# A fourth block of 250 nodes through the first dense layer inside the edge loop of a GNN and expert kernel

## The chip, the core and the metric

One core of one Trainium2 chip runs the whole program. The time is the device time of one launch in microseconds (us). Three runs of the kernel before gave 595.5, 597.15 and 599.0 us, median 597.15.

## The reference

1250 nodes with 512 numbers each, 21250 edges sorted by destination (20000 drawn, and one loop per node: 17 edges a node), 64 numbers per edge. What the change concerns is the graph layer:

```python
msg = relu(x[src] + edge_attr @ W_e + b_e)          # x is layer-normalised
aggr = segment_sum(msg, dst)
h = (1.0 + eps) * x + aggr
h = silu(batchnorm(h @ W1 + b1))                    # 512 -> 1024, statistics over all nodes
h = h @ W2 + b2                                     # 1024 -> 512
h = silu(batchnorm(h))
```

The result is added to x. Then a layer norm, a softmax gate over 16 experts, for each expert its best 156 tokens, two dense layers of 512 by 512 with a gelu between them, and a weighted scatter-add follow.

## The kernel before, in words

**Ahead of the loop** the nodes are normalised, written to a table in memory (`node_rows`) and turned into columns: `aggT` holds 4 x 128 features by 1250 nodes and starts as (1 + eps) x.

**The edge loop** takes 167 tiles of 128 edges in 56 steps (0 to 55) of three tiles (`step` on each engine, `SB` = 56). For every tile POOL issues one gather of 128 source rows (line 487) into a ring of 26 rows. PE multiplies the edge attributes in float16 halves (line 1348), two tiles at a time and two pairs ahead. DVE adds the gathered row (line 982). ACT takes the Relu into `msg` (line 615). PE folds the messages into a window of 32 nodes with a one-hot matrix (line 1327, eight instructions a tile). After a step ACT copies the sum (line 593), PE turns it (line 1336) and DVE adds it into `aggT` at the window's place (line 933, "the accumulate"; that of step i is made in step i + 1). Every 3.3 steps edge attributes are rounded to their high half on ACT (line 587) and to their low half on DVE (line 955), which lets SP load the next ones.

**Blocks of the first dense layer.** Since edges are sorted by destination, the first nodes are finished early. Three blocks of 250 nodes are multiplied by W1 inside the loop. `ZSTART` names the step in which a block's columns of `aggT` are split into float16 halves: high on ACT (`part_high`, line 600), low on DVE (`part_low`, line 965), each an instruction of 1000 columns, behind the step's other work. From the next step on, in the steps of `part_at`, PE makes one product each (`part_product`, 12 matmuls of 250 columns, line 1357; one of 8 groups of 128 output features), behind the fold of the step's second tile. One step later (`ZLAG`) ACT copies it out of PSUM with the bias (line 605) and DVE takes the statistics (line 971). `ZOFF` spreads the eight products over ten steps. W1's own halves are made in the four steps from `W1_FIRST` = `ZSTART[0] - 6`.

**Whether the nodes are finished** is guarded by `SLOPE` and `OFFSET`. An assert demands ZSTART x SLOPE - OFFSET to cover the block. In the kernel, DVE compares every step's smallest destination with step x SLOPE - OFFSET (lines 859 and 868). If one is below, the loop runs 41 times instead of once.

**After the loop** the last chunk of nodes, `CH[2]`, passes the first layer: ACT rounds it (line 664), PE runs 32 high matmuls over 8 banks (line 1401) and then 64 others, feature group by feature group (line 1407). ACT copies each group out (`add_bias_1`, line 641), DVE takes statistics and combines them (`z1_statistics`, lines 1014 and 1015). In between, the halves of W2 are made (ACT line 645, DVE line 1007); SP issues W2's load when the last gathered row has been used (line 418). After five of the eight groups ACT takes a square root (line 651), DVE computes the coefficients, and the silus begin (`silu_1`, line 658). They go by chunks: eight feature groups of `CH[0]`, of `CH[1]`, of `CH[2]`. DVE splits each (`split_h1`, lines 1033 and 1035).

**The second dense layer** goes chunk by chunk, 96 matmuls each (also line 1357, in the helper `product`; operands `big` and `pair` instead of `rows_z`), 3 x 32 x (sum of columns) in all. Chunk 0 takes feature groups as they come; the other two go output by output. DVE adds the bias and takes statistics (`bias_2`, lines 1042 and 1045). The rest (second silu, gate, choice of tokens, 16 experts) begins behind the last of them.

The orders on all queues are written out by hand.

Of the kernel before, what the change touches and what calls it, by code (L numbers as in the profile page):

```python
# [22 lines left out]
def gnn_ffn_kernel(nc, E, x, src, dst, dst_rows, edge_attr, W_e, b_e, W1, b1, g1, beta1, W2, b2, g2, beta2, eps,  # L23
# [6 lines left out]
    HK = H // 128  # L30
    T = -(-E // Q)
    NP = -(-T // 2)
    SB = -(-T // J)
# [8 lines left out]
    F1 = H2 // 128  # L42
# [2 lines left out]
    KH = K // 2  # L45
    LN_EPS = BN_EPS = 1e-5
    W_SCALE = 64.0
    CH = [(0, 375), (375, 375), (750, 500)]
    ZC = 250
    ZPARTS = 3  # L50
    SLOPE, OFFSET = 21.5, 14.0
    ZSTART = (13, 24, 36)
    ZOFF = (0, 1, 2, 4, 5, 6, 8, 9)
    ZLAG = 1
    assert all(s * SLOPE - OFFSET >= (c + 1) * ZC for c, s in enumerate(ZSTART))
    part_at = {ZSTART[q // F1] + 1 + ZOFF[q % F1]: q for q in range(ZPARTS * F1)}
    assert max(part_at) + ZLAG < SB and all(max(ZOFF) + 1 + ZLAG + s <= z for s, z in zip(ZSTART, ZSTART[1:]))
    W1_FIRST = ZSTART[0] - 6
    YC = [(0, 250), (250, 375), (625, 625)]
    SOON = 5  # L60
# [33 lines left out]
    with ExitStack() as ctx:  # L94
        def sb(name, shape, dt):
            return ctx.enter_context(nc.sbuf_tensor(name, shape, dt))
# [30 lines left out]
        xs_home = sb("xs_home", [128, NT * H], F32)  # L127
        xs = xs_home[0:P, :].rearrange("p (t h) -> p t h", t=NT)
        rows_z2 = sb("rows_z2", [128, NT * H], F32)
        aggT = sb("aggT", [128, HK, NPAD], F32)  # L130
# [4 lines left out]
        raw = [sb(f"raw{b}", [128, 2, HK * H], F32) for b in range(2)]  # L135
# [51 lines left out]
        colB = sb("colB", [128, 2 * EX * HK], F32)  # L187
        st1 = sb("st1", [128, F1, 1 + ZPARTS, 6], F32)
        mv1 = sb("mv1", [128, F1, 2], F32)
# [44 lines left out]
        gat = sb("gat", [KH, EX, 2], F32)  # L234
        gat_high = [sb(f"gat_high{b}", [KH, 2], F32) for b in range(2)]

        silu = [aggT[:, i, 0:CH[2][1]] for i in range(HK)]


        half = MR * H  # L240
# [14 lines left out]
        o = 0  # L255
# [16 lines left out]
        for b in range(YR):  # L272
# [4 lines left out]

        h16 = pair16[0][:].rearrange("p w a h -> p (w a h)")[:, 0:2 * HK * CH[2][1]].rearrange(
            "p (w k n) -> p w k n", w=2, k=HK)
        part16 = rows_z2[:, HK * H2:HK * H2 + HK * ZC].bitcast(F16).rearrange("p (w k n) -> p w k n", w=2, k=HK)  # L280
        z1_parts = [xs_home[:, f * ZPARTS * ZC:(f + 1) * ZPARTS * ZC] for f in range(6)]
        z1_parts += [raw[1][:].rearrange("p a w -> p (a w)")[:, f * ZPARTS * ZC:(f + 1) * ZPARTS * ZC] for f in range(F1 - 6)]

        def z1_of(f, n0, nn):

            return z1_parts[f][:, n0:n0 + nn] if n0 < ZPARTS * ZC else z1T[:, f, n0:n0 + nn]

# [244 lines left out]
        def _(act):  # L532
# [65 lines left out]
            def part_high(w, c):  # L598
                act.wait_ge(acc_done, 1 + w * SB + ZSTART[c])
                act.activation(part16[:, 0, :, :], aggT[:, :, c * ZC:(c + 1) * ZC], ACT.Copy).then_inc(part_hi, 1)  # L600

            def part_copy(w, q):
                c, f = divmod(q, F1)
                act.wait_ge(part_ps, w * (ZPARTS * F1) + (q + 1))
                act.activation(z1_parts[f][:, c * ZC:(c + 1) * ZC], bank[PB + q % 2][:, 0:ZC], ACT.Identity,
                               scale=1.0 / W_SCALE, bias=b1c[:, f:f + 1]).then_inc(part_sb, 1)

            def step(w, i):
# [3 lines left out]
                for j, t in enumerate(tiles_of(i)):  # L612
# [8 lines left out]
                    if j == min(1, last) and i - ZLAG in part_at:  # L621
                        part_copy(w, part_at[i - ZLAG])
                if i in ZSTART:
                    part_high(w, ZSTART.index(i))
# [13 lines left out]
            def add_bias_1(f):  # L638
                n0, nn = CH[2]
                act.wait_ge(z1_ps, f + 1)  # L640
                act.activation(z1T[:, f, n0:n0 + nn], bank[f][:, 0:nn], ACT.Identity,
                               scale=1.0 / W_SCALE, bias=b1c[:, f:f + 1]).then_inc(z1_sb, 1)
# [10 lines left out]
            def silu_1(q):  # L653
                (n0, nn), f = CH[q // F1], q % F1
                act.wait_ge(bn1_ready, 1 if f < SOON else 2)
                if q >= 4:
                    act.wait_ge(h1_lo, q - 3)
                act.activation(silu[q % 4][:, 0:nn], z1_of(f, n0, nn), ACT.Silu,
                               scale=bn_sc[:, 0, f:f + 1], bias=bn_bi[:, 0, f:f + 1]).then_inc(h1_ready, 1)

            n0, nn = CH[2]
            act.wait_ge(acc_done, 1 + n_pass * SB)
# [127 lines left out]
        def _(dve):  # L790
# [209 lines left out]

            n0, nn = CH[2]
            dve.wait_ge(h_hi, HK)
# [621 lines left out]
```

## Time and profile before

| | |
|---|---|
| median of three runs | 597.15 us |
| profiled execution | 595.17 us, its span 593.3 us |
| PE busy | 468.5 us, 79% of the span |
| DVE busy | 391.9 us, 66% |
| ACT busy | 320.9 us, 54% |
| POOL busy | 252.1 us, 42% |
| PE's share of the chain that ended last | 64% |
| line 1357, operands in `rows_z` (blocks in the loop) | 38.0 us, 288 matmuls |
| mean granted TensorE clock | 0.881 |

The profile is of one execution, and all places in time below are microseconds from its span's start. The edge loop lies between about 37 and 262 us, the last first-layer chunk from 262.6, the second layer from 286.8 to 338. A share of busy time is an average over stages with different limits, so the stages have to be read one by one. The granted clock is a share of full speed (2.4 GHz): 0.5 is 1.2 GHz, and a number between them is a mean over a stretch with both.

### The profile page before, as it was taken

To read this page: it belongs to the slowest core of one execution; us is meant where nothing else is said; L and a number is where in the kernel's file an instruction comes from. 1 tells how busy PE (TensorE), PEld (TensorE's weight loads), DVE (VectorE), ACT (ScalarE), POOL (GpSimd) and SP (SyncE) were. 2 spreads that over 40 slices of the span, in tenths; PEclk is the share of its full clock that TensorE was granted. 3 is DMA by queue.
4 is the path that set the end of the run, shared out by engine and by line. 5 is a ranking of instruction groups with operands and counts; after the bars stand their busy time and mean duration, and the time that the engine had idled before them with its cause. 6 is when DMAs were issued, how large, how long until landed. Compare 5 with 4: busy or idle time off the path is not lost.

```text
span 593.3 us, 13288 instructions
## 1 busy us (share of the span) xinstructions
PE 468.5 (79%) x4679; PEld 313.7 (53%) x4679; DVE 391.9 (66%) x1005; ACT 320.9 (54%) x682; POOL 252.1 (42%) x245
## 2 busy tenths in 40 slices
PE   1566778987998898879999758304799999999990
PEld 1412222443443444224565356203799999999980
DVE  5956667776677777855797476676567676766430
ACT  3634555655566566654851095432166666666660
POOL 1077777777777777300000000000635555556331
PEclk9977857999899899989999967655699999999996
DMA  9769777777777777534764047700289999974331
GB/s 223 226 188 362 243 212 227 234 243 229 230 234 234 234 227 233 169 130 156 277 170 154 0 143 215 273 0 1 73 270 272 295 268 302 257 198 76 45 44 22
DMA packets 48982, 112.54 MB, mean 190 GB/s; under 512 B 7154, under 2 KB 7630, under 8 KB 48917
## 3 DMA queue, kind: packets, MB, share of 16 engines
q0 software_dynamic: 18992, 54.02, 33.2%
q1 hardware_dynamic: 29399, 57.16, 30.0%
q8 instruction: 38, 0.62, 0.4%
q10 hardware_dynamic: 526, 0.51, 0.4%
q14 instruction: 27, 0.22, 0.1%
HBM read 98.88 MB, written 12.79 MB: 188 GB/s over the span
## 4 chain that ended last, share of the span: by engine, by line
PE 64%; DVE 13%; ACT 9%; issue 5%; DMA 3%; POOL 2%; DVEq 2%; SPq 0%; ACTq 0%; POOLq 0%
PE bank L1357 23%; PE bank L1538 12%; PE bank L1348 7%; PE bank L1327 6%; DVE bank L982 3%; PE bank L1564 2%; ACT big L615 2%; PE bank L1336 2%; PE bank L1401 2%; PE bank L1528 2%; PE bank L1519 2%; DMA xs_home<-in_x 2%; DVE rows_z L1178 1%; PE bank L1407 1%; ACT rows_z L693 1%
## 5 line engine op out<-in xcount | busy, mean ns | idle before, releaser
L615 ACT ACTIVATE big<-bank 128x512 f32<-128x512 f32 x167 | 99.9, 598 | 79.9 <-DVE bank L982 73.6
L497 POOL DMA_INDIRECT big<-token_rows,idx x32 | 37.0, 1158 | 205.9 <-DVE idx L1236 198.5
L1357 PE MATMUL bank<-big,pair 128*128 128x156 f16 (+2 forms) x1056 | 106.5, 260 | 1.1 <-DVE big L1035 0.9
L487 POOL DMA_INDIRECT pair<-node_rows,edge_home x97 | 94.0, 969 | 29.6 <-issue 27.7
L1327 PE MATMUL bank<-big,edge_home 128*32 128x128 f32 x1336 | 73.9, 307 | 36.1 <-ACT big L615 35.5
L1357 PEld LDWEIGHTS bank<-big,pair 128*128 128x128 f16 x1056 | 80.9, 97 | 24.6 <-issue 1.4
L487 POOL DMA_INDIRECT big<-node_rows,edge_home x70 | 68.6, 979 | 49.7 <-issue 47.3
L1348 PE MATMUL bank<-edge_home 64*128 64x512 f16 x501 | 78.5, 424 | 3.1 <-DVE edge_home L955 3.1
L1327 PEld LDWEIGHTS bank<-big,edge_home 128*32 128x32 f32 x1336 | 28.7, 114 | 80.9 <-issue 54.5
L506 POOL DMA_INDIRECT out<-rows_z,idx x32 | 51.0, 1593 | 45.1 <-issue 26.1
L982 DVE TENSOR_TENSOR bank<-pair,bank 128x512 f32<-128x512 f32 x97 | 64.9, 688 | 6.8 <-PE bank L1348 4.9
L982 DVE TENSOR_TENSOR bank<-big,bank 128x512 f32<-128x512 f32 x70 | 46.9, 688 | 10.6 <-DMA big<-node_rows,edge_home 6.9
L744 ACT ACTIVATE big<-bank,colB 128x156 f32<-128x156 f32 x64 | 21.5, 387 | 45.7 <-PE bank L1538 45.7
L1357 PE MATMUL bank<-rows_z 128*128 128x250 f16 x288 | 38.0, 284 | 0.0
L1348 PEld LDWEIGHTS bank<-edge_home 64*128 64x128 f16 x501 | 19.0, 99 | 35.2 <-issue 23.8
L1357 PEld LDWEIGHTS bank<-rows_z 128*128 128x128 f16 x288 | 27.4, 102 | 11.6 <-issue 6.6
L933 DVE TENSOR_TENSOR aggT<-bank,aggT 128x128 f32 x56 | 16.3, 291 | 25.2 <-PE bank L1336 20.9
L1538 PE MATMUL bank<-big,raw 128*128 128x156 f32 x192 | 29.6, 311 | 0.5 <-ACT big L738 0.5
L1224 DVE TENSOR_SCALAR big<-iota_slot,slot 125x156 f16<-125x156 f16 x160 | 28.8, 265 | 0.0
L1538 PEld LDWEIGHTS bank<-big,raw 128*128 128x128 f32 x192 | 27.7, 201 | 0.8 <-ACT big L738 0.8
L948 DVE SCALAR_TENSOR_TENSOR edge_home<-iota_win,edge_home 128x96 f32<-128x96 f32 (+1 forms) x56 | 17.7, 316 | 15.0 <-PE bank L1327 14.5
L593 ACT ACTIVATE fold_sum<-bank 128x128 f32<-128x128 f32 x56 | 15.4, 275 | 18.6 <-PE bank L1327 18.3
(222 smaller groups left out, 769.9 us busy)
## 6 DMA issues: line engine op xcount, KB each, us to landing
raw<-in_L_ffn_w SPq DMA_DIRECT2D x12, 1024.0 KB, 8.6
edge_home<-in_L_ffn_w SPq DMA_DIRECT2D x6, 1024.0 KB, 9.5
pair<-in_L_ffn_w SPq DMA_DIRECT2D x6, 1024.0 KB, 9.6
edge_home<-in_edge_attr SPq DMA_DIRECT2D x19, 320.0 KB
xs_home<-in_x SPq DMA_DIRECT2D x10, 448.0 KB
xs_home<-in_L_ffn_w SPq DMA_DIRECT2D x4, 1024.0 KB, 8.4
aggT<-in_L_ffn_w SPq DMA_DIRECT2D x4, 1024.0 KB, 9.7
node_rows<-xs_home SPq DMA_DIRECT2D x5, 448.0 KB
```

The lines of the kernel that those rows point to most:

```text
L487: pool.indirect_dma_start(row(t), None, node_rows, bass.IndirectOffsetOnAxis(src_i[:, t:t + 1], 0)).then_inc(row_in[t % RR], 16)
L497: pool.indirect_dma_start(xg[e % XR][:, a, :], None, token_rows, bass.IndirectOffsetOnAxis(idx[:, e, a:a + 1], 0)).then_inc(xg_in[e % XR], 16)
L506: pool.indirect_dma_start(out, bass.IndirectOffsetOnAxis(idx[:, e, a:a + 1], 0), yw[e % YR][:, a, :], None, compute_op=ALU.add).then_inc(y ...
L615: act.activation(msg[:, t % MR, :], bank[t % PB][0:Q, :], ACT.Relu, scale=1.0 / E_SCALE).then_inc(msg_ready, 1)
L744: act.activation(h32[e % 2][:, f, :], bank[2 + half][:, f % 2 * K:(f % 2 + 1) * K], ACT.Gelu_apprx_tanh, bias=colB[:, e * HK + f:e * HK + ...
L948: dve.scalar_tensor_tensor(out=onehot[i % 2][:, 0:n, :], in0=iota_win[:].unsqueeze(1).to_broadcast([Q, n, WIN]), scalar=shift[:, i:i + 1], ...
L982: dve.tensor_tensor(bank[t % PB][0:Q, :], row(t), bank[t % PB][0:Q, :], ALU.add).then_inc(row_used, 1)
L1224: last = dve.tensor_scalar(pick[e % 2][:, t, :], iota_slot[:], slot[:, e, t:t + 1], None, ALU.is_equal)
L1327: done = pe.matmul(bank[6 + b][a * WIN:(a + 1) * WIN, 0:HB], onehot[b][:, j, :], msg[:, t % MR, a * HB:(a + 1) * HB], start=(j == 0), stop ...
L1348: last = pe.matmul(bank[t % PB][0:Q, :], attr16[u % 2][side, i, c * Q:(c + 1) * Q], We16[side, j, :], start=(p == 0), stop=(p == 2), skip_ ...
L1357: last = pe.matmul(bk, weights(i, k), values(j, k), start=(begin and p == k == 0), stop=(end and p == 2 and k == n - 1), skip_group_check= ...
L1538: last = pe.matmul(bank[2 + half][:, f % 2 * K:(f % 2 + 1) * K], e32[e % RH][:, 0, k, f * 128:(f + 1) * 128], xT[e % 2][:, k, :], start=(k ...
```

## The change

A fourth block (nodes 750 to 999) is split in step 46, multiplied in steps 47 to 54 without pauses and copied in steps 48 to 55. Blocks 0 and 2 start one step earlier (12 and 35), and with block 0 the halves of W1 (steps 6 to 9 in place of 7 to 10). The chunk after the loop has 250 nodes instead of 500; in the second layer the chunks have 500, 500 and 250 columns instead of 375, 375 and 500. `SLOPE` rises to 22.1, which the earlier starts need. The blocks' results take 1000 columns per feature group; five groups lie in `xs_home` and three in `raw[1]`.

```diff
-    CH = [(0, 375), (375, 375), (750, 500)]
+    CH = [(0, 500), (500, 500), (1000, 250)]
     ZC = 250
-    ZPARTS = 3
-    SLOPE, OFFSET = 21.5, 14.0
-    ZSTART = (13, 24, 36)
-    ZOFF = (0, 1, 2, 4, 5, 6, 8, 9)
+    ZPARTS = 4
+    SLOPE, OFFSET = 22.1, 14.0
+    ZSTART = (12, 24, 35, 46)
+    ZOFF = ((0, 1, 2, 4, 5, 6, 8, 9),) * 3 + (tuple(range(8)),)
     ZLAG = 1
     assert all(s * SLOPE - OFFSET >= (c + 1) * ZC for c, s in enumerate(ZSTART))
-    part_at = {ZSTART[q // F1] + 1 + ZOFF[q % F1]: q for q in range(ZPARTS * F1)}
-    assert max(part_at) + ZLAG < SB and all(max(ZOFF) + 1 + ZLAG + s <= z for s, z in zip(ZSTART, ZSTART[1:]))
+    part_at = {ZSTART[q // F1] + 1 + ZOFF[q // F1][q % F1]: q for q in range(ZPARTS * F1)}
+    assert max(part_at) + ZLAG < SB and all(max(o) + 1 + ZLAG + s <= z for o, s, z in zip(ZOFF, ZSTART, ZSTART[1:]))
     W1_FIRST = ZSTART[0] - 6
...
-        silu = [aggT[:, i, 0:CH[2][1]] for i in range(HK)]
+        silu = [aggT[:, i, 0:CH[0][1]] for i in range(HK)]
...
-        z1_parts = [xs_home[:, f * ZPARTS * ZC:(f + 1) * ZPARTS * ZC] for f in range(6)]
-        z1_parts += [raw[1][:].rearrange("p a w -> p (a w)")[:, f * ZPARTS * ZC:(f + 1) * ZPARTS * ZC] for f in range(F1 - 6)]
+        z1_parts = [xs_home[:, f * ZPARTS * ZC:(f + 1) * ZPARTS * ZC] for f in range(5)]
+        z1_parts += [raw[1][:].rearrange("p a w -> p (a w)")[:, f * ZPARTS * ZC:(f + 1) * ZPARTS * ZC] for f in range(F1 - 5)]
```

## Rows read from the trace of the kernel before

**Rows 1.** Windows by stage: bounds; length, PE, PEld, DVE, ACT, POOL busy; clock, DMA, GB/s.

```profile
36.60:262.40 225.80, 188.75 (x2161) 82.29 (x2161) 161.51 (x325) 131.01 (x270) 157.97 (x163) 0.88 0.74 229
262.40:286.80 24.40, 23.30 (x96) 9.96 (x97) 14.16 (x28) 13.51 (x25) 0.00 (x0) 0.88 0.46 164
286.80:338.00 51.20, 51.18 (x288) 27.90 (x288) 36.06 (x79) 20.29 (x30) 0.00 (x0) 1.00 0.53 168
```

**Rows 2.** Timeline, last gather and last accumulate: start, length, instruction, [idle before, releaser].

```profile
243.01 0.95 POOL L487 DMA_INDIRECT pair<-node_rows,edge_home  x1 [0.30 <-issue]
...
261.59 0.29 DVE L933 TENSOR_TENSOR aggT<-bank,aggT 128x128 f32 x1 [0.83 <-PE bank L1336]
```

**Rows 3.** Windows of the loop between accumulates: steps 13-23, 24-34, 35-46, 47-54.

```profile
97.12:141.76 44.64, 39.39 (x477) 19.48 (x470) 32.59 (x66) 26.55 (x57) 33.97 (x36) 0.96 0.76 232
141.76:188.34 46.58, 41.32 (x477) 19.89 (x473) 33.27 (x68) 27.27 (x58) 35.60 (x37) 0.93 0.77 231
188.34:236.18 47.84, 42.04 (x512) 20.63 (x504) 35.16 (x72) 27.93 (x60) 36.26 (x39) 0.96 0.78 232
236.18:260.31 24.13, 19.42 (x267) 7.22 (x263) 19.80 (x41) 16.39 (x34) 5.95 (x7) 1.00 0.36 114
```

**Rows 4.** Timeline at the start of the third block, step 36.

```profile
191.50 1.03 ACT L600 ACTIVATE rows_z<-aggT 128x1000 f16<-128x1000 f32 x1
...
195.13 0.43 PE L1327 MATMUL bank<-big,edge_home 128*32 128x128 f32 x8 [2.67 <-ACT big L615]
...
196.98 2.68 PE L1357 MATMUL bank<-rows_z 128*128 128x250 f16 x12
```

**Rows 5.** Windows at a low granted clock (third number from the end).

```profile
146.00:152.60 6.60, 6.60 (x47) 2.92 (x49) 2.45 (x6) 1.94 (x6) 5.08 (x6) 0.52 0.73 204
...
197.10:200.50 3.40, 3.40 (x24) 1.92 (x25) 2.02 (x4) 0.72 (x3) 2.49 (x4) 0.56 0.74 207
...
262.00:268.70 6.70, 6.11 (x16) 2.30 (x17) 2.24 (x1) 2.07 (x4) 0.00 (x0) 0.53 0.92 309
...
340.50:350.50 10.00, 6.43 (x27) 5.83 (x28) 6.62 (x41) 9.96 (x17) 0.00 (x0) 0.51 0.25 76
```

**Rows 6.** The chain of waits: start, length, what; a product, the root, the second layer.

```profile
202.71 1.41 PE bank L1357 x12
...
282.57 0.21 ACT bn_sd L651
...
286.81 51.19 PE bank L1357 x288
```

**Rows 7.** Groups by line and form: busy us, mean ns of one, idle before.

```profile
L605 ACT ACTIVATE xs_home<-bank,colA 128x250 f32<-128x250 f32 x18 | 8.5, 474 | 0.0
L971 DVE BATCH_NORM_STATS2 st<-xs_home 128x6 f32<-128x250 f32 x18 | 7.4, 410 | 0.0
...
L1035 DVE TENSOR_TENSOR big<-aggT,big 128x375 f16<-128x375 f32 x16 | 8.8, 549 | 0.5
L658 ACT ACTIVATE aggT<-xs_home,bn_bi,bn_sc 128x375 f32<-128x375 f32 x12 | 7.8, 692 | 0.4 <-DVE big L1035 0.2
L658 ACT ACTIVATE aggT<-big,bn_bi,bn_sc 128x500 f32<-128x500 f32 x8 | 6.4, 805 | 5.6 <-DVE big L1035 5.3
...
L1035 DVE TENSOR_TENSOR big<-aggT,big 128x500 f16<-128x500 f32 x8 | 5.4, 679 | 0.3
...
L641 ACT ACTIVATE big<-bank,colA 128x500 f32<-128x500 f32 x8 | 5.4, 673 | 5.6 <-PE bank L1407 5.6
```

**Rows 8.** Timeline after the loop: W2's halves, statistics of groups 3 and 4.

```profile
268.82 1.67 ACT L645 ACTIVATE pair<-raw 128x512 f16<-128x512 f32 x3 [4.76 <-DMA raw<-in_L_gnn_W]
269.49 1.90 DVE L1007 SCALAR_TENSOR_TENSOR pair<-raw,pair 128x512 f16<-128x512 f32 x3 [3.15 <-ACT pair L645]
...
279.86 0.68 DVE L1014 BATCH_NORM_STATS2 st<-big 128x6 f32<-128x500 f32 x1 [0.17 <-ACT big L641]
...
281.56 0.68 DVE L1014 BATCH_NORM_STATS2 st<-big 128x6 f32<-128x500 f32 x1 [0.17 <-ACT big L641]
```

## The prediction

> **What bounds the kernel now.** The page came first: PE is busy 79% of the span, the most of any engine, but none is full, so the shares alone decide nothing. The windows by stage [rows 1] show the edge loop (225.8 us, PE busy 188.8), the last first-layer chunk (24.4, PE 23.3) and the second layer (51.2, PE 51.18); some 255 us follow that the change doesn't touch. Two of these stages are PE's alone. The loop is a ring of PE, DVE and ACT.
>
> Gathers fill POOL in the loop. The last starts at 243.01 us, 18.6 ahead of the last accumulate at 261.59 [rows 2], so the loop's end does not wait for POOL. The ring of 26 rows does not hold POOL up either: its last gather needs 141 rows used, and these are used before step 47, ahead of the new products.
>
> The loop is then read in stretches cut at starts of line 933's accumulates [rows 3]. The first three hold one block each (eight products and their start): 11, 11 and 12 steps in 44.64, 46.58 and 47.84 us. The fourth is eight steps, 47 to 54, with no product now: 24.13 us, 3.02 each, PE busy 19.42. PE thus has 4.7 us of idle time there.
>
> How a block starts is seen at 191 us [rows 4]. ACT rounds the block's columns (1.03 us), DVE waits for it and takes the low half, the additions queue behind that on DVE, and ACT's Relu behind them. PE stands 2.67 us. Then the granted clock falls: 0.56 in 197.1 to 200.5, and 0.52 in 146.0 to 152.6 after the block before [rows 5], near the level of 1.2 GHz. The first product takes 2.68 us [rows 4] in place of 1.41 [rows 6].
>
> **The change, part by part.**
>
> 1. *Block 3 in steps 46 to 54.* The direct price is that of the blocks already there, less plain steps at 3.02 us: 44.64 - 11 x 3.02 = 11.4; 46.58 - 11 x 3.02 = 13.4; 47.84 - 12 x 3.02 = 11.6 [rows 3]. I take **+11.5**, the value of two of the three. The copies (0.47 on ACT) and statistics (0.41 on DVE) [rows 7] are in it. Eight products of 1.41 are 11.3 us of PE work [rows 6]; if they filled all 4.7 us of PE's idle time and the start cost nothing, the price would be 6.6. That is the lower end. It excludes a gain, because PE has to do the work. The upper end is 13.4. Behind the waiting DVE and ACT stand only the additions and Relus that are priced here. SP gets its edge loads' releases from DVE later, as in the older blocks, where nothing waits for them. POOL has no wait added.
>
> 2. *Blocks 0 and 2 and W1's halves one step earlier.* The work is the same, and no wait for W1's load shows in the waits from 40 to 100 us. Taken at zero, within 1 either way; a clock that falls at other places can be worth about that much, as 11.4 against 13.4 shows.
>
> 3. *The chunk after the loop, 250 columns for 500.* PE's own part is now 23.3 us [rows 1], from 262.6 to 285.9. After: 32 high products at the low clock (0.53 in 262.0 to 268.7 [rows 5]), 250/1.2 = 208 ns each, are 6.7 us; 64 at 117.5 ns (1.41/12 [rows 6]) are 7.5. PE would end at 276.8, 9.1 earlier. But the second layer does not start by PE. It needs the first silu, that needs five features' statistics, and those share DVE with W2's halves. W2's load is issued when the last row is used, whatever the chunk's width; ACT waits 4.76 us for it until 268.82, and DVE's first three low halves end at 271.39 [rows 8]. From there DVE does per feature a statistic, an aggregate and a low half. The spacing is now 1.70 us, of which it waits 0.17: 1.53 of work [rows 8]. A statistic of 250 columns takes 0.41 [rows 7] against 0.68 [rows 8], so 1.26. Feature 4's begins at 271.4 + 4 x 1.26 = 276.4, and the root 0.74 later (1.01 now, 281.56 to 282.57 [rows 6, 8], less 0.27) at 277.2, against 282.57. From the root to the second layer's first product is 4.24 us now [rows 6]. The bias copy in it shrinks by 0.20; silu and subtraction of 500 columns for 375 cost 0.11 and 0.13 more [rows 7], and the cast about half of that: 4.35. So the second layer starts at 281.5 against 286.81: **-5.3**. Of PE's 9.1 us, 3.8 turn into waiting. The ends are -4 (a DVE pace of 1.53 kept) and -9.1.
>
> 4. *The clock at that start.* PE would stand from 276.8 to 281.5, 4.7 us, where it now stands 0.9 (285.9 to 286.81). After the second layer it now stands from 338.0, and in 340.5 to 350.5 the granted clock is 0.51 [rows 5]. I expect it down at the new start. The low stretches in [rows 5] are 3.4, 6.6, 6.7 and 10 us long; 3.4 us at half rate lose 1.7, 6.7 lose 3.4, no fall 0. I take **+2.3**.
>
> 5. *The second layer's columns.* Their sum is the same, 96 x 1250. Now 288 products take 51.19 us [rows 6], 50.0 of them columns at 2.4 GHz: 4 ns each on top. A product of 250 columns takes 117.5 ns in the loop, 9 more than 104.2 + 4. So 96 x 9 ns = **+0.9**, between 0 and 1.3. DVE's supply holds: of its split of 500 columns the subtraction, the longer half, takes 0.68 us [rows 7], while PE uses them in 2.5.
>
> The Trainium skill, "TensorE: Matmul & The Clock Gate", section "Wait — 56ns, not 53.3ns?", puts back-to-back products at their columns over 2.4 GHz and about 2.5 ns. By it a product of 250 columns would be 106.7 ns, and the forecast some 2 us lower. The trace disagrees here, with 117.5.
>
> 6. *The tail.* The last bias and statistic behind PE's last product are of 250 columns: 0.27 less for the statistic, about as much for the bias. **-0.5**.
>
> Sum: 11.5 - 5.3 + 2.3 + 0.9 - 0.5 = **+8.9 us**. Against the profiled execution's 595.17 us: **604.1**. That execution is 2.0 below the median of 597.15; the range has this on its upper side.
>
> **The rivals.**
>
> *A. As summed*, 604.1.
>
> *B. PE's idle time takes up more of the block.* For it: eight products in a row leave fewer gaps than the older pattern, which has two pauses, and POOL is done by 244. Against: three blocks agree within 2 us, pauses included. With 6.6 for the products, 2.1 for the start (2.67 less 0.6, the idle time that a plain step has anyway: 4.7/8) and no fall of the clock ahead of the second layer: 6.6 + 2.1 - 5.3 + 0.9 - 0.5 = +3.8, 599.0.
>
> *C. Faster: W2 does not hold the second layer back.* Its place is DVE between 268.8 and the first silu. If W2's halves moved out of the way and PE's whole 9.1 came back, PE would have no time to stand and cool. With the loop at its lower end: 6.6 - 9.1 + 0.9 - 0.5 = -2.1, 593.1. It passes -0.5% only where the block costs under 5.7 us, which is less than PE's work allows. Against it: ACT's 4.76 us wait for W2 is plain, and nothing moves that load.
>
> *D. Worse:* the block costs 13.4 and the second layer starts in a low stretch of 6.7 us: 13.4 - 5.3 + 3.4 + 0.9 - 0.5 = +11.9, 607.1.
>
> *E. The change doesn't do what it says, for this input.* The kernel compares each step's smallest node with 22.1 i - 14 and, where one is below, runs the loop 41 times, at 225.8 us each [rows 1]. With 17 edges a node, a step of 384 edges advances 22.6 nodes; in the reference's own index list the nearest step is 12.8 nodes clear. Practically excluded.
>
> **How the numbers follow.** A 0.57, B 0.22, C 0.06, D 0.14, E 0.01. About 3 us (0.5%) is what a measurement of this kernel can tell from no change. Faster by more: the outer part of C and luck with the clock in the loop, 0.04. Within 0.5%: the rest of C and under half of B, 0.10. Slower: 0.86. The range goes from a little under B (598.5) to D plus the 2 us between this execution and the median (609).
>
> **What would show it.** Right: the accumulates of steps 46 and 54 about 31 us apart in place of 24.1, and the last at 272 to 274; PE standing 2.5 to 3 us at the new block's start; the second layer's first product 19 to 20 us after the last accumulate in place of 25.2, with 4 to 5 us of PE standing ahead of it and a granted clock near 0.5 behind it; that layer 53 to 55 us long; everything behind it shifted and otherwise the same. Wrong: a loop longer by under 8 us (B), a second layer that starts 16 us after the loop (C), or a third chunk that starves PE.

## The result, and the profile after

| | us |
|---|---|
| before, median of 21 runs | 596.41 |
| changed kernel, median of 21 runs | 598.86 |
| ratio | 1.0031, 95% interval 1.0015 to 1.0046 |
| profiled execution of the changed kernel | 597.08 (span 595.3) |

The change costs 0.3%, some 1.9 us by the ratio. The forecast was +8.9 us and 604.1 (range 598.5 to 609). The sign was right and the size far too large. In single executions the times reach from 595.5 to 602.4 us, so two profiles can't settle 2 us; below, medians and ratios decide between kernels, and the traces say where the time of one execution lies. All kernels are compared with runs of the kernel before that were made beside them. A ratio is turned into us with 596.4. A "stand" is a time in which PE waits, and a "low stretch" is one in which the granted clock is near 0.5.

The windows of the changed kernel between accumulates: steps 24 to 34 (to be set against the second of [rows 3], 46.58 us), 46 to 54, and 47 to 54 (the fourth of [rows 3]).

```profile
141.38:186.84 45.46, 40.22 (x481) 19.75 (x474) 33.04 (x67) 27.36 (x58) 34.80 (x36) 0.96 0.78 232
...
230.84:268.22 37.38, 33.48 (x388) 17.46 (x382) 26.29 (x55) 21.64 (x47) 14.15 (x15) 0.95 0.45 133
236.39:268.22 31.83, 31.08 (x359) 16.59 (x351) 22.44 (x48) 18.37 (x41) 9.82 (x11) 0.95 0.41 123
```

Steps 47 to 54 take 31.83 us where they took 24.13, and PE is busy 31.08 of them: of its 4.7 us of idle time there 0.75 are left. With step 46 it is 37.38 against 27.71 (232.60 to 260.31 before), 9.7 more. The last accumulate is only 8.0 later than in [rows 2], because that of step 45 stands 1.8 us earlier.

The timeline at the start of the fourth block, step 46, and the last accumulate of the loop.

```profile
231.17 1.04 ACT L600 ACTIVATE rows_z<-aggT 128x1000 f16<-128x1000 f32 x1 [0.23 <-DVE aggT L933]
232.24 1.20 DVE L965 TENSOR_TENSOR rows_z<-aggT,rows_z 128x1000 f16<-128x1000 f32 x1 [0.78 <-ACT rows_z L600]
...
234.80 0.43 PE L1327 MATMUL bank<-big,edge_home 128*32 128x128 f32 x8 [3.15 <-ACT big L615]
...
236.77 2.68 PE L1357 MATMUL bank<-rows_z 128*128 128x250 f16 x12
...
269.61 0.29 DVE L933 TENSOR_TENSOR aggT<-bank,aggT 128x128 f32 x1 [0.46 <-PE bank L1336]
```

It is the picture of [rows 4] again. PE stands 3.15 us, and the first product takes 2.68 us, at the lower clock.

The chain of waits behind the loop.

```profile
269.94 5.44 DMA raw<-in_L_gnn_W
275.40 0.64 ACT pair L645
276.06 1.90 DVE pair L1007 x3
...
283.43 0.21 ACT bn_sd L651
...
287.51 52.58 PE bank L1357 x288
```

Before, this chain led over PE from 262.6 to 280.9. Now it leads over W2's load and DVE, as argued in step 3 of the prediction. The second layer begins 17.90 us after the last accumulate (269.61), where it was 25.22 (261.59 to 286.81): 7.3 us come back, not 5.3.

PE's idle time ahead of that layer, and the clock in its windows.

```profile
287.51 3.07 PE L1357 MATMUL bank<-big,pair 128*128 128x500 f16 x7 [5.02 <-DVE big L1035]
```

```profile
288.00:291.30 3.30, 3.30 (x11) 1.23 (x10) 3.20 (x8) 2.48 (x4) 0.00 (x0) 0.59 1.01 379
291.30:329.50 38.20, 38.20 (x183) 17.54 (x181) 27.72 (x60) 16.83 (x25) 0.00 (x0) 1.00 0.60 188
```

PE stands 5.02 us, and one low stretch of the clock follows. The layer takes 52.58 us against 51.19.

### The profile page after: what moved, and what is told of

It reads as the page before. It is cut to its first block, busy times and chain, and to the rows that moved or that the text cites. A ratio compares the mean times of both kernels' runs of the same rounds, so it can differ in the third digit from the quotient of the medians.

```text
span 595.3 us, 13521 instructions
## 1 busy us (share of the span) xinstructions
PE 467.6 (79%) x4775; PEld 323.5 (54%) x4775; DVE 393.3 (66%) x1014; ACT 321.7 (54%) x691; POOL 256.4 (43%) x245
## 4 chain that ended last, share of the span: by engine, by line
PE 61%; DVE 13%; ACT 8%; issue 6%; DMA 5%; POOL 3%; DVEq 2%; SPq 1%; POOLq 0%; ACTq 0%
PE bank L1357 25%; PE bank L1538 12%; PE bank L1348 7%; PE bank L1327 6%; DVE bank L982 3%; PE bank L1564 2%; ACT big L615 2%; DMA xs_home<-in_x 2%; PE bank L1528 2%; PE bank L1519 2%; PE bank L1336 2%; DVE rows_z L1178 1%; POOL big L487 1%; ACT rows_z L693 1%; DMA pair<-node_rows,edge_home 1%
## 5 line engine op out<-in xcount | busy, mean ns | idle before, releaser
L1357 PE MATMUL bank<-big,pair 128*128 128x156 f16 (+2 forms) x1056 | 107.9, 261 | 5.2 <-DVE big L1035 5.0
L487 POOL DMA_INDIRECT pair<-node_rows,edge_home x97 | 96.6, 996 | 29.5 <-issue 27.1
L1327 PE MATMUL bank<-big,edge_home 128*32 128x128 f32 x1336 | 72.4, 302 | 34.6 <-ACT big L615 33.9
L487 POOL DMA_INDIRECT big<-node_rows,edge_home x70 | 70.0, 1000 | 51.0 <-issue 49.5
L1348 PE MATMUL bank<-edge_home 64*128 64x512 f16 x501 | 76.8, 416 | 3.2 <-DVE edge_home L955 3.2
L506 POOL DMA_INDIRECT out<-rows_z,idx x32 | 51.6, 1612 | 44.2 <-issue 25.2
L1357 PE MATMUL bank<-rows_z 128*128 128x250 f16 x384 | 51.7, 288 | 0.0
L1357 PEld LDWEIGHTS bank<-rows_z 128*128 128x128 f16 x384 | 37.0, 103 | 15.8 <-issue 8.6
## 6 DMA issues: line engine op xcount, KB each, us to landing
aggT<-in_L_ffn_w SPq DMA_DIRECT2D x4, 1024.0 KB, 10.3
```

Source lines behind the costliest of these rows:

```text
L487: pool.indirect_dma_start(row(t), None, node_rows, bass.IndirectOffsetOnAxis(src_i[:, t:t + 1], 0)).then_inc(row_in[t % RR], 16)
L506: pool.indirect_dma_start(out, bass.IndirectOffsetOnAxis(idx[:, e, a:a + 1], 0), yw[e % YR][:, a, :], None, compute_op=ALU.add).then_inc(y ...
L1327: done = pe.matmul(bank[6 + b][a * WIN:(a + 1) * WIN, 0:HB], onehot[b][:, j, :], msg[:, t % MR, a * HB:(a + 1) * HB], start=(j == 0), stop ...
L1348: last = pe.matmul(bank[t % PB][0:Q, :], attr16[u % 2][side, i, c * Q:(c + 1) * Q], We16[side, j, :], start=(p == 0), stop=(p == 2), skip_ ...
L1357: last = pe.matmul(bk, weights(i, k), values(j, k), start=(begin and p == k == 0), stop=(end and p == 2 and k == n - 1), skip_group_check= ...
```

## The experiments

Medians by kernel, each with its ratio to the kernel before:

| kernel | median us | ratio (95% interval) |
|---|---|---|
| shift_only | 593.76 | 0.9950 (0.9922 to 0.9978) |
| block0_early | 593.53 | 0.9950 (0.9924 to 0.9975) |
| block2_early | 595.95 | 0.9991 (0.9968 to 1.0015) |
| w1_early | 596.06 | 0.9992 (0.9971 to 1.0013) |
| offsets_8 | 593.04 | 0.9938 (0.9915 to 0.9961) |
| thin_products | 592.09 | 0.9918 (0.9896 to 0.9940) |
| tiny_split | 595.36 | 0.9978 (0.9953 to 1.0003) |
| post_only | 590.02 | 0.9895 (0.9859 to 0.9930) |
| w2_early | 595.74 | 0.9969 (0.9948 to 0.9990) |
| shift_w2 | 594.07 | 0.9958 (0.9930 to 0.9986) |
| keep_warm | 596.58 | 0.9999 (0.9973 to 1.0025) |
| late_low | 586.95 | 0.9848 (0.9808 to 0.9888) |
| late_low_8 | 588.03 | 0.9856 (0.9814 to 0.9897) |
| late_low_4 | 582.25 | 0.9758 (0.9723 to 0.9793) |

**The earlier starts alone.**

```diff
-    SLOPE, OFFSET = 21.5, 14.0
-    ZSTART = (13, 24, 36)
+    SLOPE, OFFSET = 22.1, 14.0
+    ZSTART = (12, 24, 35)
```

> The kernel before with the earlier starts alone: blocks at steps 12, 24 and 35, W1's halves from step 6, SLOPE 22.1; three blocks and the old chunks. Theory 1 (the block in the loop costs about 10 us, the two stages behind it return about 7 to 8, and the earlier starts are worth nothing of themselves): within 1 us of before. Rival 2 (in the two profiles the accumulate of step 45 stands 1.8 us earlier, so the earlier starts are a gain of their own that hid part of the block's price): 1.5 to 2 us faster than before.

3.0 us faster than before, more than the rival's 1.5 to 2. The rival holds: the change contains a gain that the prediction took at zero. Two kernels took it apart, with starts at (12, 24, 36) and at (13, 24, 35).

> Starts at 12, 24, 36 in the kernel before: only block 0 and W1's halves one step earlier. shift_only was 3 us faster than before. If the gain is from the first block and W1 (one more step without a product between blocks 0 and 1, so that the start of block 1 costs one low stretch of the clock instead of two): 1.5 to 3 us faster than before. If it is from block 2: within 1 us.

> Starts at 13, 24, 35 in the kernel before: only block 2 one step earlier. If the gain of shift_only is from the first block: within 1 us of before. If it is from block 2 (one more plain step at the loop's end, other places for the edge halves): 1.5 to 3 us faster.

The whole gain is with block 0, none that can be measured with block 2. W1's halves move with block 0, so they were moved alone (`W1_FIRST = ZSTART[0] - 7` in the kernel before).

> The kernel before with W1's halves alone one step earlier (steps 6 to 9), blocks at 13, 24, 36. block0_early was 2.4 to 3 us faster than before. If the gain is W1's (its rounding falls where DVE waited for gathers): 2 to 3 us faster than before. If it is the block's (an extra step without product between blocks 0 and 1): within 1 us of before.

No difference. What is left is block 0 itself. One candidate is the place of its products before block 1's start in step 24. Starting at 13, the last product is in step 23; starting at 12, in 22. The next kernel keeps the starts and draws the products together, which gives the same free step. It does so in all three blocks, not in block 0 alone.

```diff
-    ZOFF = (0, 1, 2, 4, 5, 6, 8, 9)
+    ZOFF = (0, 1, 2, 4, 5, 6, 7, 8)
```

> The kernel before with the eight products of each block in nine steps (offsets 0,1,2,4,5,6,7,8) instead of ten; starts unchanged. If the gain of block0_early comes from the free step between block 0's last copy and block 1's start at step 24 (in the traces the start of block 1 is followed by a low stretch of 6.8 us with starts at 13, and of 3.4 us with 12): 1.5 to 3 us faster than before, and the low stretch after 146 us is 3.4 long. If it comes from W1 or from where the products meet the edge halves: within 1 us.

3.7 us faster than before. Its windows of steps 24 and 25, behind the low stretch, and in it:

```profile
139.30:150.69 11.39, 8.38 (x92) 3.50 (x86) 6.86 (x13) 5.83 (x12) 8.86 (x9) 0.85 0.76 228
147.90:151.30 3.40, 3.40 (x44) 1.36 (x43) 1.63 (x5) 1.72 (x4) 2.49 (x4) 1.00 0.78 222
144.50:147.70 3.20, 3.20 (x23) 1.51 (x20) 1.49 (x3) 1.03 (x2) 2.44 (x3) 0.57 0.72 204
```

Steps 24 and 25 take 11.39 us here and 12.57 in the kernel before. The granted clock is back at 1.00 after 3.4 us, where it stayed low for 6.6 in [rows 5]. PE's stand is the same in both (3.01 and 3.04 us). With block 0 from step 13 and ten steps, the traces show the longer low stretch (before, block2_early, w1_early), and in the nine of kernels with start 12 and the old split it is 3.4 us. The two steps are best taken together with the three ahead of them. The windows of steps 21 to 25 in w1_early, block0_early and offsets_8:

```profile
130.33:154.93 24.60, 20.77 (x207) 9.22 (x209) 15.11 (x32) 12.53 (x26) 18.64 (x20) 0.79 0.77 235
...
131.00:152.34 21.34, 17.76 (x206) 8.43 (x206) 14.73 (x31) 12.59 (x26) 16.34 (x17) 0.92 0.77 231
...
129.53:150.69 21.16, 17.58 (x205) 8.00 (x204) 14.96 (x32) 12.42 (x26) 16.19 (x17) 0.92 0.78 236
```

They take 23.1, 24.3 and 24.6 us in the three traces of the old pattern, 21.3 to 21.4 in the nine, and 21.2 in offsets_8. So the free step is worth 1.8 to 3.4 us at that place.

It is not shown that the 3.7 us of the medians come from there. In the trace of offsets_8 PE stands 1.62 us at 183.5, ahead of the third block, and the clock falls there as well:

```profile
185.50:188.80 3.30, 3.30 (x37) 1.03 (x31) 2.37 (x5) 1.85 (x4) 2.69 (x3) 0.59 0.73 220
```

Steps 35 and 36 take 9.89 us for 8.36 before, and from the accumulate of step 13 to the last one the loop is only 0.3 us shorter than before (159.06 for 159.32). Behind the loop, the second layer starts 25.2 to 25.3 us after the last accumulate in the three traces of the old pattern, and 22.4 to 24.1 in block0_early, shift_only, shift_w2 and offsets_8, by how much of the 32 high products falls into a low stretch. One trace each can't tell whether that belongs to the edit or to the execution; it stays open.

**What the fourth block costs, and which part of it.** First its matmuls: 1 of 12 is left in each product of that block, the other eleven are left out.

```diff
+                if c == 3:
+                    pe.matmul(bank[PB + q % 2][:, 0:ZC], W1_16[:, 0, 0, f * 128:(f + 1) * 128], part16[:, 0, 0, :],
+                              start=True, stop=True, skip_group_check=True).then_inc(part_ps, 1)
+                    return
```

> The changed kernel with the eight products of the fourth block cut from 12 matmuls to 1 (11/12 of the product left out; split, copies and statistics stay). It takes 10.3 us of PE work out of steps 47 to 54. Theory 1 (PE was idle for 4.7 us there, so the products pay for two thirds of their work): 6 to 8 us faster than the changed kernel, 4 to 6 faster than before, the start's price left in the loop. Rival (the block's price is in the copies and statistics on ACT and DVE and in the split, the matmuls fit in beside): under 3 us faster than the changed kernel.

6.8 us faster than the changed kernel (592.09 to 598.86), two thirds of the 10.3 us of PE work. The 4.7 us of idle time would leave 5.6, and the trace has that in the loop: 31.72 us for 37.38 in steps 46 to 54. It gives 2.0 of it back behind the loop, where the second layer starts 19.9 us after the last accumulate for 17.9. So the medians show more than the traces, and why is not known.

Then its split: the rounding is done on 2 of 250 columns of each of the 4 groups, on ACT and in the same way on DVE, and left out on the rest.

```diff
+                nn = 2 if c == 3 else ZC
...
-                act.activation(part16[:, 0, :, :], aggT[:, :, c * ZC:(c + 1) * ZC], ACT.Copy).then_inc(part_hi, 1)
+                act.activation(part16[:, 0, :, 0:nn], aggT[:, :, c * ZC:c * ZC + nn], ACT.Copy).then_inc(part_hi, 1)
```

> The changed kernel with the split of the fourth block (step 46, one instruction on ACT and one on DVE, 1000 columns each) cut to 8 columns; the products run on what stands there. It leaves out the rounding of that block. Theory 1 (the start costs about 3 us: 2.7 to 3.2 us of PE standing less what it stands anyway, and a fall of the clock): 2 to 3.5 us faster than the changed kernel, PE's stand at that place under 1 us and the granted clock at 1 there. Rival (PE makes up for the stand later): under 1 us.

3.5 us faster than the changed kernel by the medians, 3.2 by the ratios. The window over the first product:

```profile
236.00:240.00 4.00, 4.00 (x50) 2.07 (x49) 3.36 (x8) 2.32 (x5) 3.01 (x4) 1.00 0.73 221
```

No fall of the clock. PE's stand is 1.40 us instead of 3.15, not under 1 as expected. Steps 46 to 54 in the traces of post_only (below), thin_products and tiny_split:

```profile
231.19:258.54 27.35, 21.58 (x296) 8.13 (x294) 22.10 (x46) 17.94 (x38) 13.54 (x14) 1.00 0.58 171
...
231.68:263.40 31.72, 24.91 (x308) 9.05 (x302) 25.47 (x54) 20.90 (x47) 12.31 (x13) 0.95 0.46 137
...
230.62:264.76 34.14, 31.99 (x388) 16.83 (x382) 25.19 (x55) 20.81 (x47) 13.41 (x15) 1.00 0.50 147
```

With the block whole they take 37.38, so in the loop it costs 10.0 us, of which leaving out the matmuls takes 5.7 and leaving out the split 3.2.

Last, the whole block: three blocks in the loop, the new chunks behind it. Nodes 750 to 999 never pass the first layer; their columns are read from the block before them.

```diff
-            return z1_parts[f][:, n0:n0 + nn] if n0 < ZPARTS * ZC else z1T[:, f, n0:n0 + nn]
+            return z1_parts[f][:, n0 // 2:n0 // 2 + nn] if n0 < 1000 else z1T[:, f, n0:n0 + nn]
```

> The shifted starts with three blocks and the new chunks behind the loop: nodes 750 to 999 never pass the first layer (their columns are read from the block before them, so a fifth of the first layer is left out). It shows what the two stages behind the loop return by themselves, against shift_only's 593.8 us. Theory 1 (the second layer waits for W2 and DVE, and starts with a fall of the clock): 5 us faster than shift_only, 588 to 590, with PE standing about 5 us ahead of the second layer. Rival 2 (PE's whole 9 us come back): 584 to 586.

The ratios give the block at 1.0031 - 0.9895 = 1.36%, 8.1 us, and the stages behind the loop a gain of 0.9950 - 0.9895, 3.3 us. The intervals make them about 8.1 ± 2.3 and 3.3 ± 2.7: rival 2's 9 is excluded, theory 1's 5 is not. The timeline shows why the return can be below 5:

```profile
257.97 3.65 SPq L422 DMA_DIRECT2D raw<-in_L_gnn_W  x8
...
259.82 0.29 DVE L933 TENSOR_TENSOR aggT<-bank,aggT 128x128 f32 x1 [0.84 <-PE bank L1336]
...
279.81 1.41 PE L1357 MATMUL bank<-big,pair 128*128 128x500 f16 x3 [7.32 <-DVE big L1035]
```

W2's load goes out 1.85 us ahead of the last accumulate, and PE then stands 7.32 us. In the changed kernel PE is the late engine at the loop's end and DVE uses the last row earlier, so the load goes out 2.89 ahead:

```profile
266.72 3.66 SPq L422 DMA_DIRECT2D raw<-in_L_gnn_W  x8
```

So the fourth block delays the loop's end more than it delays W2's load. By the profiles it gives back 2.1 us of its own price (17.90 against 19.99 us from the last accumulate to the second layer).

**W2's wait.** The load goes out when W1's halves are made, and all halves of W2 come ahead of the first statistics.

```diff
-            sp.wait_ge(row_used, 1 + n_pass * T)
-            for u in range(AR):
-                sp.wait_ge(attr_in[u], n_pass * (16 * uses(u, AR, NU)) + 16)
+            sp.wait_ge(W1_lo, n_pass * HK)
             for h in range(F1):
                 sp.dma_start(W2_raw[:, h * H:(h + 1) * H], W2_t[:, h, :]).then_inc(w2_in, 16)
+            sp.wait_ge(row_used, 1 + n_pass * T)
+            for u in range(AR):
+                sp.wait_ge(attr_in[u], n_pass * (16 * uses(u, AR, NU)) + 16)
...
-            for f in range(3):
+            for f in range(F1):
                 W2_low(f)
             for f in range(SOON):
                 z1_statistics(f)
-                if f < SOON - 1:
-                    W2_low(3 + f)
```

> The changed kernel with W2's load issued when W1's halves are made instead of when the last row is used (some 14 us earlier, behind the last edge loads), and all of W2's halves made ahead of the first statistics. Theory 1 (behind the loop the second layer waits for W2 and for DVE's halves, not for PE): the second layer's first matmul comes 2 to 3 us sooner after the last accumulate, PE stands about 2.6 us ahead of it in place of 5.0, perhaps with no fall of the clock; 2 to 4 us faster than the changed kernel. Rival (the wait for W2 is hidden anyway, the silu's chain sets the start): under 0.5 us; or slower, if the 2 MB of the load delay the last gathers.

> shift_only (three blocks, the old chunk of 500 behind the loop) with W2's load and halves early, as in w2_early. Theory 1: in that kernel PE works until 0.9 us before the second layer, so W2 is hidden and the change is worth under 1 us: 593 to 594. Rival (W2 holds both): 3 us faster than shift_only, as it was with the fourth block, 590.5.

With the small chunk it is worth 3.7 us (0.9969 against 1.0031), with the old chunk nothing that can be measured (0.9958 against 0.9950, to within some 2.4 us). The trace of w2_early agrees:

```profile
288.27 1.01 PE L1354 MATMUL bank<-big,pair 128*128 128x500 f16 x4 [2.80 <-DVE big L1035]
```

The second layer starts 15.7 us after the last accumulate instead of 17.9, PE stands 2.80 us ahead of it, the clock stays up and the layer takes 51.02 us. In shift_w2 the distance is 24.1 us, as in shift_only (23.8). So W2 holds the second layer back only after the change. That was step 3's claim.

**The clock ahead of the second layer.**

```diff
+            pe.wait_ge(z1_sb, 1)
+            for _ in range(22):
+                pe.matmul(bank[0][:, 0:500], W1_16[:, 0, 0, 0:128], W1_16[:, 0, 1, 0:500],
+                          start=True, stop=True, skip_group_check=True)
             pe.wait_ge(W2_lo, F1)
```

> The changed kernel with 22 matmuls of 500 columns that write a free bank between the first layer's last and the second layer's first product, 4.7 us of work where PE stood 5.0 us (their results are thrown away). Theory 1 (the stand pulls the clock down for 3.4 us, which costs the second layer 1.4 to 1.7 us): the second layer takes 51.2 us instead of 52.6, 1 to 1.7 us faster than the changed kernel. Rival (the clock falls of the loop's thin end, not of the stand): no change.

Faster than the changed kernel by 1.9 us, a little more than expected; the two intervals leave 0.1 to 3.7. The chain of waits shows the layer without a slow part, where it was 52.58 us:

```profile
288.32 51.03 PE bank L1357 x288
```

**A cheaper start.** The low half on DVE is cut in two instructions (`part_low` now takes two of the four groups), and they go behind the first and the second addition of the next step.

```diff
-                if i in ZSTART:
-                    part_low(w, ZSTART.index(i))
...
                         columns_hot(w, i + 1)
+                    if j <= 1 and i - 1 in ZSTART:
+                        part_low(w, ZSTART.index(i - 1), j)
```

> block0_early (three blocks at 12, 24, 36) with the low half of each block's split moved: two halves on DVE, behind the first and the second addition of the next step, instead of one instruction ahead of them. Theory 1 (a block's start costs about 3 us because additions, Relus and then PE stand behind the split, and the clock falls): PE's stand at a start under 1 us in place of 2.7 to 3.0, no low stretch there, 1.5 to 3 us a block, so 5 to 8 us faster than block0_early's 593.5. Rival (the work of the split itself, 1.0 and 1.2 us, is what costs): under 1.5 us in all.

6.6 us faster than block0_early (6.1 by the ratios), 9.1 than before, with the same arithmetic. The timeline at the start of its third block:

```profile
183.53 1.03 ACT L600 ACTIVATE rows_z<-aggT 128x1000 f16<-128x1000 f32 x1
...
184.59 0.68 DVE L966 TENSOR_TENSOR rows_z<-aggT,rows_z 128x500 f16<-128x500 f32 x1 [0.54 <-ACT rows_z L600]
...
185.17 0.43 PE L1328 MATMUL bank<-big,edge_home 128*32 128x128 f32 x8 [0.68 <-ACT big L615]
...
186.92 1.48 PE L1358 MATMUL bank<-rows_z 128*128 128x250 f16 x12
```

PE stands 0.68 us for 2.67, and the product takes 1.48 us. At the start of the second block the stand is 1.22, a little over the expected 1; no low stretch follows any of the three starts.

**Both repairs together, and the fourth block judged again.**

> The changed kernel (four blocks) with both repairs: the low halves in the next step as in late_low, W2 early as in w2_early. Theory 1 (with cheap starts and W2 out of the way the fourth block costs its matmuls, 6 to 7 us, and the stages behind it return 6 to 7): within 2 us of late_low's 587. Rival (the fourth block is a loss by its PE work even so): 590 or more. Second rival (it was the starts and W2 alone that made it lose): 584 or less.

> late_low with the products of each block in nine steps instead of ten, which gave offsets_8 3 us. Theory 1 (that gain was a low stretch of the clock at the start of block 1, and late_low has none left to save): within 1 us of late_low's 587. Rival (the closer products are a gain of their own): 584 or less.

The four-block kernel with both repairs is the fastest of all, 582.25 us: 14.4 us faster than before and 4.7 faster than late_low, with intervals that do not overlap. Theory 1 falls here, and the number is the second rival's. Late_low has no early W2; that this is worth nothing with the old chunk is known from shift_w2, not from late_low. In late_low DVE now waits for a gather, and PE with it, and the clock falls at 246.8 us:

```profile
243.23 0.69 DVE L983 TENSOR_TENSOR bank<-big,bank 128x512 f32<-128x512 f32 x1 [2.00 <-DMA big<-node_rows,edge_home]
...
246.25 0.95 POOL L487 DMA_INDIRECT pair<-node_rows,edge_home  x1 [0.30 <-issue]
```

The three-block loop has caught up with POOL's gathers, the last of which starts at 246.25 us here and at 246.73 in late_low_4. Steps 46 to 54 take 30.36 us in late_low and 34.58 with the fourth block, 4.2 more, where it was 10.0. That the matmuls fill the wait for the gathers fits this and is not tested by itself. Some 2 us more go in steps 35 to 46, with the third start in step 35: the product there takes 2.68 us and the granted clock is 0.59 from 186.6 to 189.9, after stands of only 0.79 and 0.70 us. So late_low's repair did not keep the clock up there. The last accumulates are at 253.40 and 260.36 us, 7.0 apart, and the second layer starts 22.4 and 15.7 us after them, which returns 6.7. In late_low_4 PE stands 2.80 us ahead of it:

```profile
276.04 1.22 PE L1355 MATMUL bank<-big,pair 128*128 128x500 f16 x5 [2.80 <-DVE big L1036]
```

No fall of the clock follows, and that layer takes 51.02 us. It ends at 327.1 us, where it ends at 327.0 in late_low. So in these two executions the fourth block gains nothing up to there, and their whole difference of 2.9 us (spans of 585.2 and 582.3) lies behind, in work that the kernels share. The window of 392 to 420 us, late_low first, shows the clock and the matmuls there:

```profile
392.00:420.00 28.00, 18.43 (x141) 17.39 (x141) 15.99 (x79) 2.99 (x7) 10.57 (x8) 0.50 0.12 35
...
392.00:420.00 28.00, 18.55 (x177) 17.62 (x178) 17.04 (x82) 4.95 (x13) 10.44 (x8) 0.60 0.17 46
```

In late_low_4 the granted clock comes up earlier (415.2 us for 420.7). From the second layer's end to the span's, eleven of the sixteen traces take 255.1 to 256.7 us, and five (w1_early, block0_early, shift_only, shift_w2, late_low) 257.9 to 258.2. All seven kernels with the 250-column chunk are among the eleven. Whether that is chance, or a part of what the fourth block returns, is open, and so is where the 4.7 us of the medians lie.

late_low_8 is no faster than late_low (0.9856 and 0.9848). Drawing the products together gives nothing once the start of block 1, where offsets_8 gained, is followed by no low stretch in either. That fits a gain by the clock. It is not a clean proof: late_low_8's trace has a low stretch ahead of its third block (181.9 to 185.3 us), behind a stand of 1.63 us, as offsets_8 has; late_low's has none there.

## Why the prediction was wrong in size

The forecast's +8.9 and the measured +1.9 differ by 7.0 us. Two steps of the sum failed, about evenly: step 2, taken at nothing, and the size of step 1. By the ratios of shift_only and post_only:

| step | forecast | measured |
|---|---|---|
| 2, earlier starts | 0 | -3.0 |
| 1, block 3 in the loop | +11.5 | +8.1 |
| 3 to 6, behind the loop | -2.6 | -3.3 |
| sum | +8.9 | +1.9 |

The intervals are 1.7 us on the first row, 2.3 on the second and 2.7 on the third, either way.

1. **Step 2 failed.** It was taken at zero because "the work is the same", and measured -3.0, all of it with block 0 (shift_only, block0_early; w1_early and block2_early show none). The work is the same, but the step before block 1's start is not: block 0 from step 12 leaves it free of a product. offsets_8 does the same by another edit and gains too, and on top of late_low, where that start no longer pulls the clock down, it is worth nothing. In steps 21 to 25 this shows as 1.8 to 3.4 us and in the low stretch as 3.4 us for 6.6 to 6.8. That it is the whole of the 3.0 us is argued and not shown, as the trace of offsets_8 says. The prediction had the clue in its hands, 13.4 against 11.4 and 11.6, and took it for a matter of the clock within 1 us. The long low stretch stands in each of the three traces of that pattern with start 13.

2. **Step 1: the mechanism was right, the size too large.** The bounds of 6.6 and 13.4 hold. PE's idle time was used up (31.08 of 31.83 us busy), and at the start PE stood and the clock fell as in the older blocks. In the traces the block costs 9.7 in the loop against the kernel before and 10.0 against post_only, not 11.5. Why it is less is argued only: its eight products without a pause use PE's idle time more fully than the older pattern, which was rival B's argument. Another 2.1 come back behind the loop, because W2's load goes out further ahead of the loop's end. By the ratios, products (6.7 by thin_products) and start (3.2 by tiny_split) add up to 9.9, which the intervals allow beside 8.1; the traces give 5.7 and 3.2 of 10.0.

3. **Step 3: right in kind.** Second layer held by W2 and DVE, PE standing: shown by w2_early against shift_w2. The 5.3 came out as 7.3 in the profiles. 1.4 of the difference is W2 landing 5.79 us after the last accumulate (269.61 to 275.40) where 7.23 was carried over. The prediction took the load's lead over the loop's end as fixed. The rest is DVE's pace of 1.19 us a feature for 1.26, and 4.08 us from the root to the layer for 4.35.

4. **Step 4: right, the length of the stand by luck.** Stand 5.02 for 4.7 forecast; the clock fell; 1.4 us by the profile and 1.9 by keep_warm for 2.3. But both ends of the stand came some 2 us early. The 32 high products took 5.15 us for 6.7 and the 64 others 7.10 for 7.5, so that PE ended 12.9 us after the last accumulate for 15.2, and the layer began after 17.9 for 19.9.

5. **Step 5: wrong.** The group of the second layer's 250-column products shows it:

```profile
L1357 PE MATMUL bank<-big,pair 128*128 128x250 f16 x96 | 10.5, 269 | 0.0
```

10.5/96 = 109 ns, not 117.5, and the first layer's 64 take 7.10 us, 111 each. The 1.41 us of the chain [rows 6] are the way from a product's start to the next instruction's on PE (202.71 to 204.12), so they hold more than the product's twelve matmuls. In keep_warm, with no fall of the clock, the layer takes 51.03 us for 51.19 before: the term was about zero instead of +0.9.

The Trainium skill, "TensorE: Matmul & The Clock Gate", section "Wait — 56ns, not 53.3ns?", which the prediction set aside, was nearer than the prediction's reading: the estimate worked out from it is 106.7 ns.

6. **Step 6: as forecast** within 0.2 us: the last statistic 0.42 for 0.68 us, the bias 0.48 for 0.74.

Of the rivals, B came nearest with +3.8, and partly by luck: half of the miss is step 2, which B took at zero too, and the clock did fall ahead of the second layer, which B denied. C's mechanism, taking W2 out of the way, is no effect of the change, but is real: w2_early gets 3.7 us from it. The median of 598.86 lies just inside the range, at its low end, because the median of the kernel before lies above the execution that was profiled; the shift against before (+1.9 for +8.9) is what the forecast got wrong.

## What to carry to other kernels

Moving work into a loop pays for the engine's idle time only if its side effects do not stop the loop. Here 1.2 us of rounding on DVE, placed ahead of three additions, cost 2 us a block. Moving it behind additions gained 1.0% with three blocks (late_low against block0_early). With that, and with W2's load ahead, the kernel with the fourth block is 2.4% faster than before and 0.9% faster than late_low, where the plain change lost 0.3%. When a stage shrinks, look for what was hidden behind it: a load whose issue hangs on the old stage's end becomes the bound. And an edit that moves a pattern by a step "with the same work" has to be priced against what else stands in the steps where it now meets a stall.

## What the runs showed of the hardware

In the loop the granted clock fell to the lower level after PE had stood 2.7 to 3.2 us, at one block start after the other, and after 2.58 us at the wait for a gather in late_low. The stand's length alone does not decide it. The clock also fell after stands of 1.62 us (offsets_8, from 185.5) and of 0.79 and 0.70 us (late_low_4, from 186.6). It stayed up after 1.22 us (second block of late_low) and 1.40 us (tiny_split), and ahead of the second layer after 2.25 us (keep_warm) and 2.80 us (w2_early, late_low_4). After the start of block 1 it stayed low for 3.4 us in ten traces and 6.6 to 6.8 in three, with the same stand of 3.0 us.

From step 13 on, traces of kernels with the same loop (shift_only, shift_w2, post_only) agree within 0.1 us in most steps. Three places scatter more: with block 0 at step 12 and the old split, the accumulate of step 12 stands between 99.2 and 103.4 us, behind a stretch in which the clock changes often; the 32 high products of 500 columns behind the loop take between 6.92 and 9.87 us, by whether the clock falls there; and the granted clock comes up for the experts 87.8 to 89.8 us after the second layer's end in eleven traces and 91.5 to 93.7 in five.
